# First batch's K through three places, V weights before query weights, GpSimd's mask and residuals at other places in its order

## The chip, the cores and the metric

One core of a Trainium2 chip runs the whole kernel in one launch. The metric is the device time of that launch in microseconds (us); the kernel before is shown with the median of three runs and with one profiled execution.

## The reference, cut to what matters

Eight sequences of 100 rows x 512 attend to a context of 722 rows x 512 with 16 heads of 32. Two layers follow one another, each a cross attention and a feed-forward network:

```python
q = heads(norm(x) @ Wq.T + bq); k = heads(ctx @ Wk.T + bk); v = heads(ctx @ Wv.T + bv)
p = softmax(q @ k.T / sqrt(32) + mask)      # the mask in layer 0 only
x = x + tanh(g) * (p @ v)                   # layer 1 has an output projection Wo
x = x + tanh(g) * ffn(norm(x))              # layer 0: ternary, 512-2048-2048-2048-512; layer 1: quantized gated
```

## The kernel before

Every engine has its own program, written out by hand, with semaphores between them (`w.wait_ge(sem, n)`). Every matrix product is made of three: each operand is split in a high part (rounded to the type fp32r, on ScalarE) and a low part (what is left, a subtraction on VectorE or GpSimd), and TensorE adds high x high, high x low, low x high (`PAIRS`).

The program runs `attention(0)`, the units of the first feed-forward network, `attention(1)`, and the second network. The change is in what both `attention(L)` do before their loop over 64 pairs of heads; it is called the opening below. In it TensorE computes, one after another, jobs of 12 matmuls each:

- `K00, K01, K10, K11, K20, K21, K30`: K of batch 0 for the groups of four heads g = 0 to 3, each in two halves of the 722 columns (384 and 338). `K10` is group 1, half 0. `K31` is done later, in the loop.
- `V0` to `V4`: V of batch 0, 128 context rows each, 12 matmuls of 512 columns.
- `turn_x(b)`: the normalized input rows of sequence b, turned by four transposes; `query(half)`: the query projection of four sequences, 48 matmuls of 400 columns.

A job's result goes to one of two PSUM banks in turn (5, 7), so that a job waits until the job two before it has been read out by `low_job` (semaphore `v_job`). It is read by ScalarE (`high_job`, K also gets its bias) and then by VectorE (`low_job`). High and low part of K land in the one pair of tiles `m.kst`, from which SyncE's queue stores them to DRAM (`store_k` to `kd`); `load_k` reads them back in another layout (`KS`). Since there is one `m.kst`, the next group's `high_job` for the same half waits for the store of the last (semaphore `d_kd`):

```python
i = 4 * j[1] + j[2]
if i:
    w.wait_ge(d_kd[j[3]][(i - 1) % 4], kd_done(L, i - 1))
```

All DMAs in question are issued by SyncE in a fixed order, with its waits in between. In layer 0 that order is context and K weights (0 to 3), rest of the context, x of sequences 0 to 3, weights 4 to 7 (Wq), x of 4 to 7, weights 8 and 9 (Wv), store K00, the mask's rows, store K01, weights 10 and 11, store K10, context of batch 1, store K11, and so on. `split_w(i)` is the split of weight tile i: ScalarE's high part (line 1548), VectorE's low part (line 1099), or, for the tiles in `BY_POOL`, GpSimd's (`low_wq`, line 1966). The raw tiles sit in six places, so weight i + 6 is loaded over weight i.

The norm's statistics are `stats_x` (VectorE, lines 1258 and 1260), its roots `input_roots` (GpSimd, ten small instructions for four sequences at a time, from line 1948 to 1962), and `normal_x` (VectorE, line 1264) applies them. `mask` is prepared by GpSimd for layer 0 right at the start. In layer 1, `scaled_out` (VectorE, line 1251) and `add_residual` (GpSimd, line 1974) finish the feed-forward network's last sum while the K jobs run. Behind the query, `high_q`, `low_q` (GpSimd) and `spread_q` (twelve DMAs of SyncE, line 629) bring it to the layout in which `scores` reads it.

Of the kernel before, what the change touches and what calls it, by code (L numbers as in the profile page):

```python
# [18 lines left out]
KT = 6  # L19
# [75 lines left out]
def turned_at(i):  # L95

    if i == NP - 1:
# [121 lines left out]
def flamingo_kernel(nc, t, out):  # L219
    top = ExitStack()  # L220
    with top:
# [86 lines left out]
        for L in range(2):  # L308
# [10 lines left out]
            V = [at(f"V{z}_{L}", o[f"V{z}"], [128, KT * 2 * D], F32R) for z in range(2)]  # L319
            m.QS = at(f"QS_{L}", o["QS"], [98, 2, H, S], F32R)  # L320
# [9 lines left out]
            m.wq = [V[1][:, 2048 * c:2048 * c + 2048].rearrange("p (k n) -> p k n", k=4) for c in (0, 1)]  # L330
            m.xT = [PT[:, 1600 * c:1600 * c + 1600].rearrange("p (k n) -> p k n", k=4) for c in (0, 1)]
# [3 lines left out]
            tail = at(f"xt_{L}", o["V1"] + 16384, [128, 4, D])  # L335
# [77 lines left out]
        def wait_low_w(w, L, i):  # L413

            if i in BY_POOL:
                w.wait_ge(g_wl, 2 * L + BY_POOL.index(i) + 1)
            else:
                w.wait_ge(v_wl, 10 * L + i + 1 - (2 if i > BY_POOL[-1] else 0))

# [29 lines left out]
        def _(e):  # L449
            w = Waits(e)  # L450
            def attention(L):
# [6 lines left out]
                if L == 0:  # L458
# [24 lines left out]
                    load_k(L, m, 0, 1)  # L483
                    spread_q(L, m, 0)
                else:
# [13 lines left out]
                    store_x(5)  # L499
                    store_k(L, m, *K30[1:])  # L500
                    for n in (6, 7):
                        store_x(n)
# [7 lines left out]
                    load_k(L, m, 0, 1)  # L510
                for k in range(4):
                    load_ctx(L, m, 1, 1, k)
# [61 lines left out]
            def load_w(L, m, i):  # L574
                if i >= 6:
                    wait_low_w(w, L, i - 6)
                e.dma_start(m.stage[i % 6], t[f"{('wk', 'wq', 'wv')[i // 4]}{L}"][:, i % 4, :]).then_inc(d_w[i % 6], 16)
# [15 lines left out]
            def store_k(L, m, b, g, half):  # L593
# [6 lines left out]
                for c in range(2):  # L600
                    e.dma_start(kd[n % 4, c][:, off:off + size],
                                raw32(m.kst[c][:, off:off + size])).then_inc(d_kd[half][n % 4], 16)
# [68 lines left out]
        def _(e):  # L671
# [12 lines left out]
            def attention(L):  # L684
# [3 lines left out]
                def job(j):  # L688
# [4 lines left out]
                    for k in range(4):  # L693
                        wait_ctx(w, L, j[1], half, k)
                        wait_low_w(w, L, (0 if j[0] == "k" else 8) + k)
# [116 lines left out]
                def query(half, groups=range(4)):  # L812
                    for g in groups:
                        bank = (2, 3, 4, 6)[g]
                        w.wait_ge(v_xt, 8 * L + 4 * half + 4)
                        for k in range(4, 8):
# [18 lines left out]
                for j in (K01, K10, K11, K20, K21, K30):  # L835
# [3 lines left out]
                job(V0)  # L839
                turn_x(2)  # L840
                turn_x(3)
                job(V1)
# [3 lines left out]
                job(V2)  # L846
# [234 lines left out]
        def _(e):  # L1081
# [10 lines left out]
            def attention(L):  # L1092
                m = rooms[L]
                wlow = {0: m.wk, 1: m.wq, 2: m.wv}
# [14 lines left out]
                def low_job(j):  # L1109
                    o = job_out(m, j, ring_bank(L, j))  # L1110
                    w.wait_ge(a_job, NJOB * L + JOB[j] + 1)
                    if j[0] == "k":
                        off, n = HALF[j[3]]
                        bias = bcol(f"bk{L}", j[2])
                        e.scalar_tensor_tensor(m.kst[1][:, off:off + n], o, bias, raw32(m.kst[0][:, off:off + n]),  # L1115
# [158 lines left out]
                if L == 0:  # L1274
# [4 lines left out]
                    low_job(K00)  # L1279
                    low_job(K01)  # L1280
# [5 lines left out]
                    split_w(4)  # L1286
                    split_w(5)
                    low_job(K11)
                    low_job(K20)
                    split_w(8)  # L1290
                    split_w(9)
# [3 lines left out]
                    low_job(K30)  # L1295
                    split_w(10)
# [901 lines left out]
```

## Time and profile before

| | |
|---|---|
| median of 3 runs | 1657.96 us (1657.34 to 1658.47) |
| the profiled execution's own time | 1650.54 us |
| its span, first to last instruction | 1648.7 us |
| TensorE busy (matmul) | 1587.4 us, 96% |
| VectorE, ScalarE, GpSimd busy | 1034.7, 969.6, 394.4 us |
| mean granted TensorE clock | 0.988 of full |
| chain that ended last | TensorE 88%, VectorE 4%, ScalarE 2%, DMA 2% |

Busy is the sum of an engine's instructions. The chain is followed back from the last instruction, at each step to what released it. The granted clock is 1.00 at 2.4 GHz and 0.50 at 1.2 GHz; a figure between is a mean over the stretch. The rows on which the prediction rests are in a section of their own, further on.

### The profile page before, as it was taken

Reading aid. Unit: us, or ns where it says so; the run is one execution under the profiler, and the core shown is the slowest. Engines: PE = TensorE matmul, PEld = TensorE weight load, DVE = VectorE, ACT = ScalarE, POOL = GpSimd, SP = SyncE. Lnnn points to the kernel's source line nnn. Section 1 sums busy time; section 2 is a strip of 40 time slices with the busy share of each in tenths; the row PEclk is TensorE's granted clock in tenths of the full one; section 3 lists DMA queues with packets and bytes.
Section 4 is the critical chain, followed back from the end, with each engine's and each line's share of the span. In section 5 each row is a group of like instructions: output and inputs, shape, how many; then the busy total and the mean of one; then the engine's idle time right before and its main releaser. Section 6 shows DMA issues by size and latency. Waiting matters only on the chain.

```text
span 1648.7 us, 25635 instructions
## 1 busy us (share of the span) xinstructions
PE 1587.4 (96%) x9298; PEld 1440.2 (87%) x9298; DVE 1034.7 (63%) x1833; ACT 969.6 (59%) x2007; POOL 394.4 (24%) x540
## 2 busy tenths in 40 slices
PE   4999999999997999999999999999999999999898
PEld 4888999999987999999999997789999989998654
DVE  4477777777787453223544425547777777778786
ACT  3376777677665456454544435247667767766565
POOL 3021121221224222222222222312202120213741
PEclk8899999999999999999999999999999999999999
DMA  7457766767572224555375644366676667666400
GB/s 223 104 146 192 188 172 163 195 173 185 144 207 78 96 90 164 184 179 178 99 227 199 212 147 145 111 156 175 154 191 159 180 159 190 163 152 177 155 12 29
DMA packets 146232, 257.74 MB, mean 156 GB/s; under 512 B 40916, under 2 KB 90196, under 8 KB 145968
## 3 DMA queue, kind: packets, MB, share of 16 engines
q1 hardware_dynamic: 145648, 255.79, 55.3%
q8 instruction: 85, 1.39, 0.4%
q14 instruction: 51, 0.42, 0.1%
q10 hardware_dynamic: 448, 0.14, 0.0%
HBM read 187.46 MB, written 58.57 MB: 149 GB/s over the span
## 4 chain that ended last, share of the span: by engine, by line
PE 88%; DVE 4%; ACT 2%; DMA 2%; issue 1%; POOL 1%; SPq 1%; DVEq 0%; ACTq 0%; POOLq 0%
PE ps L998 32%; PE ps L703 16%; PE ps L699 14%; PE ps L765 8%; PE ps L753 8%; PE ps L739 2%; PE ps L742 2%; PE ps L939 2%; DMA kd<-ksl 1%; PE ps L952 1%; PE ps L825 1%; PE ps L864 1%; PE ps L741 1%; PE ps L740 1%; ACT P L1593 1%
## 5 line engine op out<-in xcount | busy, mean ns | idle before, releaser
L998 PE MATMUL ps<-ah_f,wh_f 128*128 128x400 f32 (+1 forms) x1296 | 443.7, 343 | 0.9 <-issue 0.8
L998 PE MATMUL ps<-al_f,wh_f 128*128 128x400 f32 (+1 forms) x1296 | 442.2, 342 | 0.0
L1489 DVE TENSOR_TENSOR wl_f<-raw_f,wh_f 128x1024 fp32r<-128x1024 f32 x85 | 103.8, 1223 | 239.0 <-POOL wh_f L2133 239.0
L1914 POOL TENSOR_TENSOR cxl<-raw,cxh 128x384 fp32r<-128x384 f32 (+1 forms) x112 | 105.7, 965 | 619.0 <-ACT cxh L1556 619.0
L998 PEld LDWEIGHTS ps<-ah_f,wh_f 128*128 128x128 f32 x1296 | 243.5, 188 | 2.4 <-issue 1.5
L998 PEld LDWEIGHTS ps<-al_f,wh_f 128*128 128x128 f32 x1296 | 243.9, 188 | 0.0
L1127 DVE TENSOR_REDUCE nmax<-ps 100x1 f32<-100x722 f32 x256 | 220.6, 903 | 33.0 <-PE ps L741 29.4
L1593 ACT ACTIVATE P<-ps,nmax 100x722 f32<-100x722 f32 x256 | 219.9, 861 | 31.0 <-DVE nmax L1127 30.8
L1602 ACT ACTIVATE PT<-ps 128x400 fp32r<-128x400 f32 x384 | 166.5, 505 | 78.6 <-PE ps L753 77.4
L1848 ACT ACTIVATE raw_f<-wl_f 128x1024 f32<-128x1024 f32 x88 | 93.4, 1062 | 178.9 <-DVE wl_f L1489 178.9
L1133 DVE TENSOR_TENSOR PT<-ps,PT 128x400 fp32r<-128x400 f32 x384 | 196.3, 566 | 3.2
L699 PE MATMUL ps<-cxh,wkh 128*128 128x338 f32 (+1 forms) x512 | 174.9, 342 | 22.2 <-DVE ksl L1115 11.9
L2133 POOL CAST wh_f<-raw_f 128x1024 fp32r<-128x1024 f32 x85 | 92.3, 1086 | 341.8 <-PE ps L998 339.2
L699 PE MATMUL ps<-cxh,wkl 128*128 128x338 f32 (+1 forms) x512 | 170.0, 332 | 0.0
L699 PE MATMUL ps<-cxl,wkh 128*128 128x338 f32 (+1 forms) x512 | 169.1, 330 | 0.0
L703 PE MATMUL ps<-wvh,cxh 128*128 128x512 f32 (+1 forms) x384 | 160.4, 418 | 4.8 <-DVE ksl L1115 2.7
L765 PE MATMUL ps<-PT,V 128*128 128x400 f32 (+1 forms) x768 | 162.4, 347 | 2.2 <-DVE QT L1146 1.4
L753 PE MATMUL ps<-ident,P 100*128 100x100 f32 (+1 forms) x1536 | 155.8, 252 | 5.3 <-DVE PT L1133 4.1
L753 PEld LDWEIGHTS ps<-ident,P 100*128 100x128 f32 (+1 forms) x1536 | 145.7, 139 | 16.2 <-DVE PT L1133 4.5
L1115 DVE SCALAR_TENSOR_TENSOR ksl<-ps,cols,ksh 128x384 fp32r<-128x384 f32 (+1 forms) x128 | 75.6, 591 | 134.0 <-ACT ksh L1566 133.9
L703 PE MATMUL ps<-wvh,cxl 128*128 128x512 f32 (+1 forms) x384 | 151.9, 396 | 0.0
L703 PE MATMUL ps<-wvl,cxh 128*128 128x512 f32 (+1 forms) x384 | 151.5, 395 | 0.0
(188 smaller groups left out, 2596.8 us busy)
## 6 DMA issues: line engine op xcount, KB each, us to landing
KS<-kd SPq DMA_DIRECT2D x192, 361.0 KB
raw_f<-in_h SPq DMA_DIRECT2D x64, 512.0 KB, 4.1
raw_f<-in_gud SPq DMA_DIRECT2D x48, 512.0 KB, 4.5
raw<-in_ctx SPq DMA_DIRECT2D x64, 192.0 KB, 3.7
kd<-ksh SPq DMA_DIRECT2D x64, 192.0 KB, 2.2
kd<-ksl SPq DMA_DIRECT2D x64, 192.0 KB, 2.5
raw_f<-in_w SPq DMA_DIRECT2D x24, 512.0 KB, 3.7
raw<-in_ctx SPq DMA_DIRECT2D x64, 169.0 KB, 4.4
```

The lines of the kernel that those rows point to most:

```text
L699: ins = e.matmul(o, m.wk[x][:, k, 128 * j[2]:128 * j[2] + 128], m.cx[y][:, k, off:off + n], start=(k == 0 and c == 0), stop=(k == 3 and c ...
L703: ins = e.matmul(o, m.cx[y][:, k, 128 * kt:128 * kt + KM[kt]], m.wv[x][:, k, :], start=(k == 0 and c == 0), stop=(k == 3 and c == 2))
L753: ins = e.transpose(ps[0:KM[kt], bank, o:o + S], m.P[0:S, (2 * i + h) % 3, 128 * kt:128 * kt + KM[kt]], ident[0:S, 0:S])
L765: ins = e.matmul(o, m.V[b % 2][0:r, kt, g, 128 * pr:128 * pr + 128], m.PT[0:r, i % 2, :, kt, :], start=(kt == 0), stop=(kt == KT - 1))
L998: return e.matmul(o, p, q, start=start, stop=stop)
L1127: e.tensor_reduce(m.nmax[0:S, c:c + 1], scores_of(n), AX.X, ALU.max, negate=True).then_inc(v_max, 1)
L1133: e.tensor_tensor(lo, ps[:, bank, 0:400].rearrange("p (k n) -> p k n", k=2), raw32(hi), ALU.subtract).then_inc(v_t, 1)
L1489: e.tensor_tensor(wl[:, z, :], raw[:, r, :], raw32(wh[:, z, :]), ALU.subtract).then_inc(v_ul, 1)
L1593: e.activation(m.P[0:S, n % 3, :], scores_of(n), ACT.Exp, bias=m.nmax[0:S, c:c + 1], accum_out=m.rs[0:S, r:r + 1]).then_inc(a_exp, 1)
L1602: e.activation(m.PT[:, i % 2, 0, 2 * x:2 * x + 2, :], ps[:, bank, 0:400].rearrange("p (k n) -> p k n", k=2), ACT.Copy).then_inc(a_t, 1)
L1848: e.activation(raw[:, r, :], raw32(wl[:, z, :]), ACT.Abs, accum_out=low[:, z, 0:1]).then_inc(a_raw, 1)
L1914: e.tensor_tensor(m.cx[1][:, k, off:off + n], m.raw[:, k, off:off + n], raw32(m.cx[0][:, k, off:off + n]), ALU.subtract).then_inc(g_cx, 1)
```

## The change

For batch 0 of either layer, K of groups 1 and 2 gets tiles of its own (`m.kst0`, in room that V and the turned probabilities use later), so that only `K30` waits for a store (that of group 0). The weights are numbered K, V, query instead of K, query, V, so tiles 4 to 7 are Wv and 8 to 11 Wq, and GpSimd's two are 10 and 11. TensorE's order becomes K00 K01 K10 K11 K20 K21, V0, turns 0 and 1, V1, turns 2 and 3, V2, query(0), turns 4 and 5, K30, turns 6 and 7, V3, query(1). In layer 0 ScalarE and VectorE split tiles 4 to 7 straight behind K00 and tiles 8 to 11 behind turns 0 and 1; SyncE's order there follows. GpSimd makes the mask once the first context is split (`v_cx`), and in layer 1 adds six residuals instead of four ahead of the first roots.

```diff
-FIRST = ([("k", 0, g, half) for g in range(3) for half in range(2)] + [("k", 0, 3, 0)] +
-         [("v", 0, kt) for kt in range(KT - 1)])
-K00, K01, K10, K11, K20, K21, K30, V0, V1, V2, V3, V4 = FIRST
+FIRST = ([("k", 0, g, half) for g in range(3) for half in range(2)] + [("v", 0, kt) for kt in range(3)] +
+         [("k", 0, 3, 0)] + [("v", 0, kt) for kt in range(3, KT - 1)])
+K00, K01, K10, K11, K20, K21, V0, V1, V2, K30, V3, V4 = FIRST
-ADDED = (0, 1, 2, 3, 5, 7, 4, 6)
-BY_POOL = (6, 7)
+ADDED = (0, 1, 2, 3, 4, 5, 7, 6)
+BY_POOL = (10, 11)
+            m.kst0 = [[y[:, z + 722 * c:z + 722 * c + T] for c in (0, 1)] for y, z in ((PT, 3200), (V[0], 4096))]
+        def kst_of(m, b, g):
+            return m.kst if b or g in (0, 3) else m.kst0[g - 1]
...
@@ SyncE, layer 0, behind x of 0 to 3 and weights 4 to 7
-                    for b in range(4, 8):
+                    store_k(L, m, *K00[1:])
+                    store_k(L, m, *K01[1:])
+                    for b in (4, 5):
                         load_x(m, b)
-                    load_w(L, m, 8)
-                    load_w(L, m, 9)
-                    store_k(L, m, *K00[1:])
+                    store_k(L, m, *K10[1:])
+                    for b in (6, 7):
+                        load_x(m, b)
                     for c in range(2):
                         w.wait_ge(g_mask, c + 1)
                         e.dma_start(mrow[:, c, :], raw32(m.KS[0:B, 0, c, :])).then_inc(d_mrow, 16)
-                    store_k(L, m, *K01[1:])
-                    load_w(L, m, 10)
-                    load_w(L, m, 11)
-                    store_k(L, m, *K10[1:])
-                    for k in range(4):
-                        load_ctx(L, m, 1, 0, k)
                     store_k(L, m, *K11[1:])
+                    for i in range(8, 12):
+                        load_w(L, m, i)
+                    store_k(L, m, *K20[1:])
+                    store_k(L, m, *K21[1:])
                     w.wait_ge(d_mrow, 32)
                     load_k(L, m, 0, 0)
-                    store_k(L, m, *K20[1:])
-                    store_k(L, m, *K21[1:])
-                    store_k(L, m, *K30[1:])
+                    for k in range(3):
+                        load_ctx(L, m, 1, 0, k)
                     load_k(L, m, 0, 1)
                     spread_q(L, m, 0)
+                    store_k(L, m, *K30[1:])
+                    load_ctx(L, m, 1, 0, 3)
...
@@ VectorE, layer 0
                     low_job(K00)
+                    for i in range(4, 8):
+                        split_w(i)
                     low_job(K01)
...
@@ VectorE, layer 1
-                    for i in (4, 5, 8, 9, 10, 11):
+                    for i in range(4, 10):
+                        if i == 7:
+                            w.wait_ge(p_u, 87)
                         split_w(i)
...
@@ VectorE, both layers
                     for b in range(4):
                         normal_x(b)
+                low_job(V0)
                 turned_x(0)
                 turned_x(1)
-                low_job(V0)
+                if L == 0:
+                    split_w(8)
+                    split_w(9)
+                low_job(V1)
                 turned_x(2)
                 turned_x(3)
-                low_job(V1)
                 for b in range(4, 8):
                     stats_x(b)
+                low_job(V2)
                 for b in range(4, 8):
                     normal_x(b)
...
@@ ScalarE
-                        if i:
-                            w.wait_ge(d_kd[j[3]][(i - 1) % 4], kd_done(L, i - 1))
+                        if i >= 3:
+                            last = 0 if i == 3 else i - 1
+                            w.wait_ge(d_kd[j[3]][last % 4], kd_done(L, last))
...
                 if L == 0:
                     w.wait_ge(d_const, 48)
                     high_job(K00)
+                    for i in range(4, 8):
+                        split_w(i)
+                    for j in (K01, K10, K11, K20, K21):
+                        high_job(j)
...
+                high_job(V0)
+                turned_x(0)
+                turned_x(1)
+                if L == 0:
                     for i in range(8, 12):
                         split_w(i)
+                high_job(V1)
...
@@ GpSimd
                 if L == 0:
+                    w.wait_ge(v_cx, 8)
                     w.wait_ge(d_mask, 16)
...
-                    for n in range(4):
+                    for n in range(6):
                         add_residual(n)
                     input_roots(0)
-                    for n in range(4, 8):
+                    for n in range(6, 8):
                         add_residual(n)
```

## Rows read from the trace of the kernel before

**Rows 1.** Waits, first 60 us: engine, line, releaser: us in total, times, longest.
```profile
ACT ksh L1566 <- DMA kd<-ksl: 22.2, 4, 7.3
PE ps L699 <- DVE ksl L1115: 11.5, 2, 8.1
```

**Rows 2.** Timeline of TensorE, first 70 us: start, us, what, idle before.
```profile
19.09 0.31 PE L699 MATMUL ps<-cxh,wkh 128*128 128x338 f32 x1
...
29.23 0.69 PE L699 MATMUL ps<-cxh,wkh 128*128 128x384 f32 x1 [8.13 <-DVE ksl L1115]
...
33.24 0.34 PE L699 MATMUL ps<-cxh,wkh 128*128 128x338 f32 x1
...
55.53 8.90 PE L825 MATMUL ps<-PT,V 128*128 128x400 f32 x48
```

**Rows 3.** Chain that ended last, first 120 us: start, us, what.
```profile
17.32 10.55 DMA kd<-ksl
...
68.39 0.69 PE ps L681 x8
69.09 2.80 PE ps L703 x12
...
101.03 2.10 PE ps L699 x12
```

**Rows 4.** Timeline of ScalarE, first 75 us.
```profile
14.53 0.58 ACT L1566 ACTIVATE ksh<-ps,cols 128x384 fp32r<-128x384 f32 x1
...
19.25 0.63 ACT L1548 ACTIVATE V<-QT 128x512 fp32r<-128x512 f32 x1 [1.52 <-DMA QT<-in_wq]
```

**Rows 5.** Timeline of VectorE, first 75 us.
```profile
15.14 0.62 DVE L1115 SCALAR_TENSOR_TENSOR ksl<-ps,cols,ksh 128x384 fp32r<-128x384 f32 x1
...
48.22 1.28 DVE L1099 TENSOR_TENSOR wvl<-QT,wvh 128x512 fp32r<-128x512 f32 x2
```

**Rows 6.** SyncE's issue of weights 4 to 7, in its timeline.
```profile
9.40 1.78 SPq L577 DMA_DIRECT2D QT<-in_wq x4
```

**Rows 7.** DMA issues, short stretches: KB, us to landing (weight 7, weight 9, store K00).
```profile
QT<-in_wq SPq DMA_DIRECT2D x1, 256.0 KB, 11.3
...
QT<-in_wv SPq DMA_DIRECT2D x1, 256.0 KB, 12.4
...
kd<-ksh SPq DMA_DIRECT2D x1, 192.0 KB, 8.7
```

**Rows 8.** TensorE in one stretch: us, busy, matmuls, granted clock, DMA share, GB/s.
```profile
40.00:46.60 6.60, 5.57 (x20) 0.51 1.00 243
```

**Rows 9.** TensorE's waits from 1050 to 1105 us (layer 1's opening).
```profile
PE ps L703 <- DVE ksl L1115: 2.7, 1, 2.7
...
PE ps L681 <- DVE P L1264: 0.6, 1, 0.6
PE ps L699 <- DVE ksl L1115: 0.4, 1, 0.4
```

**Rows 10.** Instructions of line 1264, `normal_x`: ns min/median/max, first and last start.
```profile
L1264 DVE TENSOR_SCALAR P<-res_f,mv,rq x4: 1479/1484/1498, 1066.5 to 1070.7; 100x512 f32<-100x512 f32 x4
L1264 DVE TENSOR_SCALAR xt<-res_f,mv,rq x4: 537/538/545, 1087.5 to 1088.9; 100x512 f32<-100x512 f32 x4
```

**Rows 11.** Timeline of GpSimd, 1050 to 1075 us.
```profile
1054.20 5.05 POOL L1974 TENSOR_TENSOR res_f<-res_f,tmp 100x512 f32<-100x512 f32 x4 [12.43 <-DVE tmp L1251]
1062.82 0.26 POOL L1948 TENSOR_SCALAR rq<-mv 100x4 f32<-100x4 f32 x1 [3.56 <-DVE mv L1260]
...
1066.42 5.51 POOL L1974 TENSOR_TENSOR res_f<-res_f,tmp 100x512 f32<-100x512 f32 x4
```

**Rows 12.** SyncE's issue of the spread query, in its timeline.
```profile
66.81 5.82 SPq L629 DMA_DIRECT2D QS<-qh x8
72.67 2.54 SPq L629 DMA_DIRECT2D QS<-ql x4
```

**Rows 13.** DMA issues from 66 to 76 us: KB, us to landing.
```profile
QS<-ql SPq DMA_DIRECT2D x4, 50.0 KB, 2.0
```

More of the change, by code:

```diff
@@ L498, in attention @@
                     store_k(L, m, *K21[1:])
-                    store_x(5)
-                    store_k(L, m, *K30[1:])
-                    for n in (6, 7):
+                    for n in range(5, 8):
                         store_x(n)
@@ L510, in attention @@
                     load_k(L, m, 0, 1)
+                    store_k(L, m, *K30[1:])
                 for k in range(4):
@@ L601, in store_k @@
                     e.dma_start(kd[n % 4, c][:, off:off + size],
-                                raw32(m.kst[c][:, off:off + size])).then_inc(d_kd[half][n % 4], 16)
+                                raw32(kst_of(m, b, g)[c][:, off:off + size])).then_inc(d_kd[half][n % 4], 16)
             def load_k(L, m, b, g):
@@ L815, in query @@
                         w.wait_ge(v_xt, 8 * L + 4 * half + 4)
-                        for k in range(4, 8):
+                        for k in range(8, 12):
                             wait_low_w(w, L, k)
@@ L834, in attention @@
                     w.wait_ge(v_res, 2)
-                for j in (K01, K10, K11, K20, K21, K30):
+                for j in (K01, K10, K11, K20, K21, V0):
                     job(j)
@@ L838, in attention @@
                 turn_x(1)
-                job(V0)
+                job(V1)
                 turn_x(2)
                 turn_x(3)
-                job(V1)
+                job(V2)
                 query(0)
@@ L845, in attention @@
                 turn_x(5)
-                job(V2)
+                job(K30)
                 turn_x(6)
@@ L1335, in attention @@
                 turned_x(5)
-                low_job(V2)
+                low_job(K30)
                 turned_x(6)
@@ L1573, in high_job @@
                         if L and j[1] == 0:
-                            w.wait_ge(g_res, B)
+                            w.wait_ge(g_res, (2, 4, 7, 8)[min(j[2], 3)])
+                        if j[1] == 0 and j[2] >= 4:
+                            for h in range(2):
+                                w.wait_ge(d_kd[h][2], kd_done(L, 2))
                         e.activation(high_columns(m, j), o.rearrange("p (g r n) -> p g r n", g=4, r=2),
@@ L1601, in high_turned @@
                             w.wait_ge(p_pv, NP * L + i - 1)
+                        if i == 1:
+                            for h in range(2):
+                                w.wait_ge(d_kd[h][1], kd_done(L, 1))
                         e.activation(m.PT[:, i % 2, 0, 2 * x:2 * x + 2, :],
@@ L1660, in high_query @@
                         w.wait_ge(p_q, 8 * L + 4 * half + g + 1)
-                        for i in (7, 11):
+                        for i in (9, 11):
                             wait_low_w(w, L, i)
@@ L1677, in attention @@
                     high_job(K00)
-                    high_job(K01)
-                    split_w(4)
-                    split_w(5)
-                    high_job(K10)
-                    split_w(6)
-                    split_w(7)
-                    high_job(K11)
-                    high_job(K20)
-                    split_w(8)
-                    split_w(9)
-                    high_job(K21)
-                    high_job(K30)
-                    split_w(10)
-                    split_w(11)
-                else:
                     for i in range(4, 8):
                         split_w(i)
-                    w.wait_ge(p_u, 87)
+                    for j in (K01, K10, K11, K20, K21):
+                        high_job(j)
+                else:
+                    for i in range(4, 12):
+                        split_w(i)
+                    for j in (K00, K01, K10, K11, K20, K21):
+                        high_job(j)
+                high_job(V0)
+                turned_x(0)
+                turned_x(1)
+                if L == 0:
                     for i in range(8, 12):
                         split_w(i)
-                    for j in (K00, K01, K10, K11, K20, K21, K30):
-                        high_job(j)
-                turned_x(0)
-                turned_x(1)
-                high_job(V0)
+                high_job(V1)
                 turned_x(2)
                 turned_x(3)
-                high_job(V1)
+                high_job(V2)
                 high_query(0)
@@ L1712, in attention @@
                 turned_x(5)
-                high_job(V2)
+                high_job(K30)
                 turned_x(6)
```

35 lines of the change are left out of this document (14 added, 21 removed).

## Prediction

> **What bounds the kernel now.** I read the page first: TensorE is busy for 96% of the span and carries 88% of the chain that ended last. So the kernel is bound by TensorE, and a change to the order around it can gain only where TensorE stands still or runs at its lower clock, or lose by making more of that. Next the waits of the first 60 us. ScalarE stood 22.2 us, in four waits, for stores of K's low part, and TensorE 11.5 us for VectorE's low part of K [rows 1]. The reader is to see one chain in these two rows: the one pair of tiles for K is not free until its store to DRAM has landed, so ScalarE can't read out the next group, so VectorE can't finish it, so the PSUM bank isn't free. TensorE's timeline shows where it hurts: K11 starts at 19.09, K20 not before 29.23 after 8.13 us of nothing, and even query(0) starts only at 55.53 [rows 2]. The chain says what was late: the store of K00, issued at 17.32, took 10.55 us [rows 3], behind the loads that were issued ahead of it. The same openings, layer 0 and layer 1, are all that the edit touches; the loops behind them are TensorE's.
>
> **Layer 0, the sum.** I compare from K11's start (19.09) to the end of V3. V3 is the row that starts at 69.09 and takes 2.80, so it ends at 71.9 [rows 3]: 52.8 us. Both orders hold the same work there. At full clock it is K11, K20, K21 and K30, 2.10 for a half of 384 columns and 338/384 of it, 1.85, for the other [rows 3], 7.9 in all; four V jobs of 2.80, 11.2; four pairs of turns at 0.69, 2.8; query(0), 8.9 [rows 2]. Sum 30.8. So 22.0 us are lost today.
>
> What is lost after the change:
> - *Waits for stores: none up to K21.* Groups 0, 1 and 2 have tiles of their own. K30 waits for K00's store, which by then is 30 us old.
> - *A new wait.* ScalarE's four splits of weights 4 to 7 now stand ahead of its reading of K01. Queued behind them are K01, K10 and K11; VectorE has the same order. Today the first of the four tiles is waited for at 19.25 already [rows 4]. The four loads are issued from 9.40 on, 0.45 apart, and nothing ahead of them in SyncE's order changes [rows 6]; the last, issued at 10.8, lands 11.3 us later, at 22.1 [rows 7]. Then ScalarE splits it (0.63 [rows 4]) and reads K01 (about the same), while VectorE takes half of 1.28 for its split and then 0.62 for K01's low part [rows 5]: K01 is done at 24.0. TensorE finishes K10 at 19.1 and needs K01's bank for K11, so it stands still for 4.9 us.
> - *Lower clock.* After 8.13 us of nothing K20 took from 29.23 to 33.24, 4.0 us instead of 2.10 [rows 2, 3]: 0.48 us are lost per us at the low level. Later the clock stood at 0.51 for 6.6 us on end although TensorE worked in 5.57 of them [rows 8]. A stall of 4.9 us lies between no fall and these; bounds 0 to 7 us, so 0 to 3.4 lost. I take 5.6 us, 2.7 lost, because the stall is nearer to the one of 8.13 and a slow stretch may also outlast one job.
> - *Small gaps* between jobs: 0.5 (0 to 1).
>
> After K11 I find nothing late: K20's bank needs K10, read right behind K01; stats and roots end before VectorE comes to the first normalized row behind K21; weights 4 to 7 are long split when V0 starts. Lost: 4.9 + 2.7 + 0.5 = 8.1, against 22.0. **Layer 0 gains 13.9 us**, and V3 ends at about 58.
>
> *Weights 8 to 11* move behind the store of K11, which waits for VectorE (28.8 by the same walk), and behind four x tiles and six K stores. Issued from 29.8 to 31.7, they must be split by ScalarE (four times 0.57) ahead of V1's reading at 39.0, and by GpSimd (1.3 each) before query(0) at 42.7. With a landing after 5 us there is a margin of 1 to 2 us, so they cost nothing; with the 11.3 of [rows 7] they would cost (rival C). x of 4 to 7 is needed at about 41 only; *the mask* is then made at 15 to 20 us, where VectorE has a hole, and its two small DMAs gate nothing before the first scores; its old place held up one low part of the context at 6.8 us, but the next K weight hadn't landed yet, so nothing is gained there. The store of K30, now behind the twelve query DMAs, serves a load two pairs later.
>
> One rule speaks on the new wait. Today four x loads and two weight loads are issued behind weights 4 to 7 and share the engines with them; after the change they come later. The store of K00 landed after 8.7 us at 25.2, ahead of weight 9, issued before it and landed after 12.4 us at about 27.4 [rows 7], so order of issue is not order of landing. The Trainium skill (DMA: Bandwidth & Descriptors, section on queues, rings and completion order) says that on each DMA engine descriptors are consumed in ring order. By that rule later loads don't hold back weight 7, and the sum stands; by the other reading weight 7 lands up to 3 us earlier (rival B).
>
> **Layer 1, the sum.** TensorE's waits are 2.7 for V0's bank, 0.6 for the second turn and 0.4 for a K bank [rows 9], 3.7 together. The first two come from `normal_x`: four of them took 1484 ns each, against 538 for the other four [rows 10], while GpSimd added residuals at 1066.42 to 1071.9 [rows 11], and V0's bank waited behind them on VectorE. After the change GpSimd adds six before the roots: 6 x 1.26 from 1054.20 is 1061.8, still ahead of the roots' start at 1062.82, which wait for VectorE [rows 11], so the two moved ones are free; two remain beside `normal_x`, and two of its four stay slow. V0 no longer stands behind them, since K21's low part comes first; the second turn waits until 1069.6 where V0 ends at 1068.1, less one turn: 0.8. **Gain 3.7 - 0.8 = 2.9** (bounds 1.0, if all four stay slow, and 3.7). VectorE's split of weight 7 now waits for unit 86 of the network before, while units 86 and 87 still keep TensorE busy: nothing.
>
> **First scores.** They need the spread query: 2.4 us from query(0)'s end (55.53 + 8.90 = 64.4) to the first issue at 66.81, 8.4 of issuing [rows 12], 2.0 to land [rows 13], 12.8 together. TensorE's cover is now two pairs of turns, K30 instead of V2, V3 and three quarters of a query: 1.4 + 2.1 + 2.8 + 6.7 = 13.0, 0.7 less than before. That is barely enough; I take 0.2 lost over both layers (0 to 2).
>
> **Total.** 13.9 + 2.9 - 0.2 = 16.6. The profiled execution's own 1650.54 becomes 1633.9; it ran 7.4 us under the median shown, so for the median 1657.96 - 16.6 = **1641.4 us**, 1.0% less. Moved work that stands in the openings is passed on in full, because from the first scores on TensorE has hardly a gap.
>
> **Rivals.**
> - **A, as worked out** (0.60): 1641.4. Its own range, from the clock (0 to 3.4), layer 1 and the first scores: 1638 to 1645.
> - **B, weights 4 to 7 land earlier** (0.14), since less is queued with them: weight 7 at about 19.5, a stall of 2.3 instead of 4.9 and a shorter slow stretch, 3.3 gained on top: 1638. For it: the landing order in [rows 7]; against it the even steps in which the four land.
> - **C, a new wait at the query weights** (0.17). They take 11.3 us like their forerunners and land at 43.0. ScalarE's splits stand ahead of V1's reading and of turns 2 and 3, so query(0) starts at 45.7 instead of 42.7, 3.0 lost, and 1.8 more if that brings a slow stretch of 3.7 us: 1646.2. For it: their issue now follows stores and x tiles that drain at the same time. Against it: by 30 us the first rush of loads is over.
> - **D, no change** (0.04): the opening gets shorter, but the first scores then wait for K or the query, or the loop's context loads come late, and the time is given back: 1658.
> - **E, slower** (0.03). Place: ScalarE's queue at weight 7, with all of K behind it. Each us that it lands later is a us lost. Weight 7 would have to land after 22.1 + 16.6 = 38.7; at 42 the time is 1661. Nothing queued ahead of it has grown, which is why I give it so little.
> - Mixtures of A and C with smaller losses hold the rest (0.02).
>
> **Range.** B's lower end and A without any slow stretch go to 1636; C with some more of D's losses to 1650. Outside lie most of D, E and a little more: two in ten at most. A measurement here tells about 0.2% (3.3 us) from nothing: faster 0.94, within it 0.03, slower 0.03.
>
> **What would show it.** Right: no wait of ScalarE for stores in the first 60 us; TensorE's only large gap from 19 to 24, ended by K01's low part; query(0) at about 43; V3's end at 58; in layer 1 `normal_x` with two slow and two fast, and three TensorE waits less. Wrong: a wait of ScalarE for the query weights near 37 to 43, a gap ahead of the first scores, or a gap at 19 that ends well before or after 24.

## The result, and the profile after

The changed kernel takes 1635.99 us (median of 4 runs: 1630.64, 1631.64, 1640.34, 1640.59) against 1657.65 us for the kernel before beside it. The ratio is 0.9868, 95% interval 0.9828 to 0.9908. Forecast was 1641.4 with a range from 1636 to 1650: the direction came out, and so did the place of the gain, but the gain is larger than forecast, and the median lies 0.01 us under the range's lower end.

The profiled execution's own time is 1640.59 us, its span 1638.8, its mean granted clock 0.986; before it was 1650.54, 1648.7 and 0.988. From its page, the busy time of each engine:

```profile
PE 1592.8 (97%) x9298; PEld 1446.9 (88%) x9298; DVE 1031.3 (63%) x1833; ACT 970.8 (59%) x2007; POOL 393.7 (24%) x540
```

The same 9298 matmuls are busy 5.4 us longer than before. That is the first sign that some of the gain of the opening was paid back at the lower clock. Waits of TensorE in the first 60 us, answering to [rows 1] (us in total, times, longest):

```profile
PE ps L704 <- DVE cxl L1111: 9.3, 2, 7.1
PE ps L704 <- DVE ksl L1121: 3.6, 1, 3.6
```

ScalarE has no wait for a store left; its waits for DMAs are now these:

```profile
ACT wvh L1554 <- DMA QT<-in_wv: 3.8, 1, 3.8
ACT cxh L1562 <- DMA raw<-in_ctx: 3.1, 4, 2.1
ACT wkh L1554 <- DMA QT<-in_wk: 1.1, 2, 0.7
ACT V L1554 <- DMA QT<-in_wq: 0.4, 1, 0.4
```

The wait of 11.5 us for K's low part [rows 1] has become one of 3.6, and what stands behind it is ScalarE's wait for weight 4. TensorE's timeline, answering to [rows 2], with the first scores (L744) as its last row:

```profile
22.68 0.65 PE L704 MATMUL ps<-cxh,wkh 128*128 128x338 f32 x1 [3.64 <-DVE ksl L1121]
...
39.86 8.90 PE L830 MATMUL ps<-PT,V 128*128 128x400 f32 x48
...
61.75 0.39 PE L744 MATMUL ps<-KS,QS 98*100 98x512 f32 x1
```

ScalarE's timeline, answering to [rows 4], shows the four splits without a pause and K01 behind them:

```profile
18.89 2.51 ACT L1554 ACTIVATE wvh<-QT 128x512 fp32r<-128x512 f32 x4 [3.82 <-DMA QT<-in_wv]
21.31 0.53 ACT L1573 ACTIVATE ksh<-ps,cols 128x338 fp32r<-128x338 f32 x1
```

query(0) starts 15.7 us earlier than in [rows 2]. Layer 0's first scores start at 61.75 instead of 78.28: **16.5 us gained**. Their position was read in both timelines; the stretches below divide the openings (columns as in [rows 8]). First the kernel before, from K11 to V3's end, and layer 1 from its first K matmul to its first scores:

```profile
19.09:71.90 52.81, 37.98 (x178) 0.81 0.53 146
1052.98:1102.11 49.13, 45.11 (x248) 1.00 0.54 144
```

Then the changed kernel, the same work:

```profile
19.04:55.36 36.32, 32.62 (x177) 0.95 0.80 198
1042.32:1088.49 46.17, 44.49 (x248) 1.00 0.54 148
```

In layer 0 TensorE stands still for 3.7 us instead of 14.8, and it is busy 5.4 us less with the same jobs, because less of them runs at the lower clock. Layer 1's opening is 3.0 us shorter. Together the openings gain 19.5 us.

But the two profiled spans differ by 9.9 us only. From layer 0's first scores to layer 1's first K matmul the changed kernel took 980.6 us (61.75 to 1042.32), the one before 974.7. The loss of 5.9 us lies where the attention loop hands over to the network. (Another 3.7 us were lost from layer 1's first scores to the end, 550.3 us against 546.6. There too it is the clock: in the four stretches of 20 us that begin 400 us behind those scores it was 0.83, 0.90, 0.93 and 0.92, before 0.91, 0.83, 1.00 and 1.00.) TensorE in the changed kernel:

```profile
480.00:500.00 20.00, 14.44 (x92) 0.84 0.07 20
500.00:520.00 20.00, 17.89 (x100) 0.76 0.34 104
520.00:540.00 20.00, 20.00 (x103) 0.89 0.29 102
```

and before, where these stages come some 15 us later:

```profile
500.00:520.00 20.00, 14.80 (x87) 0.83 0.07 21
520.00:540.00 20.00, 17.91 (x124) 1.00 0.39 130
```

Both have a pause of 2.1 us there, for the same releaser. After it the changed kernel's matmuls of 200 columns took 0.41 us each:

```profile
514.15 0.93 PE L808 MATMUL ps<-ident,x 100*128 100x100 f32 x4 [2.11 <-DVE x L1242]
...
515.10 0.41 PE L1003 MATMUL ps<-al_f,wh_f 128*128 128x200 f32 x1
```

and those of the kernel before 0.27:

```profile
529.61 0.56 PE L803 MATMUL ps<-ident,x 100*128 100x100 f32 x4 [2.10 <-DVE x L1236]
...
530.24 0.28 PE L998 MATMUL ps<-ah_f,wh_f 128*128 128x200 f32 x1
530.35 0.27 PE L998 MATMUL ps<-al_f,wh_f 128*128 128x200 f32 x1
```

It is the same pause, one time with the clock at its lower level (1.2 GHz) behind it and one time without. Nothing in the diff touches this place, so the question for the experiments is twofold: which part gives the 19.5 us, and does the clock at the hand-over belong to the change or differ from run to run.

### The profile page after: what moved, and what is told of

It is laid out like the page before. It is cut to its first block, busy times and chain, and to the rows that moved or that the text cites. A ratio compares the mean times of both kernels' runs of the same rounds, so it can differ in the third digit from the quotient of the medians.

```text
span 1638.8 us, 25637 instructions
## 1 busy us (share of the span) xinstructions
PE 1592.8 (97%) x9298; PEld 1446.9 (88%) x9298; DVE 1031.3 (63%) x1833; ACT 970.8 (59%) x2007; POOL 393.7 (24%) x540
## 4 chain that ended last, share of the span: by engine, by line
PE 92%; DVE 3%; ACT 2%; issue 1%; POOL 1%; DMA 1%; SPq 1%; DVEq 0%; ACTq 0%; POOLq 0%
PE ps L1003 32%; PE ps L708 16%; PE ps L704 15%; PE ps L758 8%; PE ps L770 8%; PE ps L830 2%; PE ps L944 2%; PE ps L744 2%; PE ps L747 2%; PE ps L957 1%; PE ps L869 1%; PE ps L746 1%; PE ps L745 1%; DMA QT<-in_wv 1%; ACT P L1603 1%
## 5 line engine op out<-in xcount | busy, mean ns | idle before, releaser
L770 PEld LDWEIGHTS ps<-PT,V 128*128 128x128 f32 (+1 forms) x768 | 141.2, 191 | 3.3 <-DVE QT L1152 0.2
```

Source lines behind the costliest of these rows:

```text
L770: ins = e.matmul(o, m.V[b % 2][0:r, kt, g, 128 * pr:128 * pr + 128], m.PT[0:r, i % 2, :, kt, :], start=(kt == 0), stop=(kt == KT - 1))
```

## Experiments

The ratio is always to the kernel before, run beside it. "First scores" is the start of layer 0's first scores in the profile (78.28 before, 61.75 changed), "opening 1" the stretch from layer 1's first K matmul to its first scores (49.13 before, 46.17 changed).

**1. The old queue behind weights 4 to 7.** The prediction let weights 4 to 7 land as late as before, because later loads were not to hold them back; rival B let them land earlier, because less is queued with them. Here the x tiles 4 to 7 and two more weights (1.3 MB) go right behind them again, as before the change:

```diff
                     for i in range(4, 8):
                         load_w(L, m, i)
+                    for b in range(4, 8):
+                        load_x(m, b)
+                    load_w(L, m, 8)
+                    load_w(L, m, 9)
                     store_k(L, m, *K00[1:])
                     store_k(L, m, *K01[1:])
-                    for b in (4, 5):
-                        load_x(m, b)
                     store_k(L, m, *K10[1:])
-                    for b in (6, 7):
-                        load_x(m, b)
...
-                    for i in range(8, 12):
+                    for i in range(10, 12):
                         load_w(L, m, i)
```

> The changed kernel, with SyncE's loads of x 4 to 7 and of weights 8 and 9 put back right behind weights 4 to 7, as in the kernel before. In the changed kernel ScalarE ran its four splits of weights 4 to 7 from 18.89 to 21.4 us without a pause, and K11 started at 22.68. Theory B (later loads hold the earlier ones back): the four splits have pauses again, the last weight lands near 22.1, K11 starts near 24.0, and the first scores come 1.3 to 3 us later than the changed kernel's 61.9. Theory A (order in the rings, later loads don't matter): splits and K11 as in the changed kernel within 0.3 us, and the earlier landing has another cause.

Measured: 1642.11 us in one run (clock 0.986); first scores at 63.34, 1.6 later. Weight 7's landing (DMA issues, KB, us to landing), first with the old queue:

```profile
QT<-in_wv SPq DMA_DIRECT2D x1, 256.0 KB, 11.3
```

and in the changed kernel:

```profile
QT<-in_wv SPq DMA_DIRECT2D x1, 256.0 KB, 9.6
```

The first of the four took 10.0 against 9.1. ScalarE's splits with the old queue:

```profile
19.76 1.26 ACT L1554 ACTIVATE wvh<-QT 128x512 fp32r<-128x512 f32 x2 [4.55 <-DMA QT<-in_wv]
21.27 0.63 ACT L1554 ACTIVATE wvh<-QT 128x512 fp32r<-128x512 f32 x1 [0.25 <-DMA QT<-in_wv]
22.42 0.63 ACT L1554 ACTIVATE wvh<-QT 128x512 fp32r<-128x512 f32 x1 [0.52 <-DMA QT<-in_wv]
```

The last split starts at 22.42, which is the sum's 22.1 plus a little, and K11 at 24.31 after 4.5 us: this is nearly the stall that the prediction worked out (24.0, 4.9). Two single traces can't size this, since landings vary from run to run. Over all 13 traces of this case, weight 7 landed after 9.5 to 10.8 us with the new order behind it (nine traces, mean 10.1) and after 10.7 to 11.3 with the old one (four traces, mean 11.1); the first of the four tiles landed after 9.1 to 10.2 and after 9.5 to 10.0, which is no clear difference. In the seven traces with the changed kernel's loads and splits K11 started at 22.50 to 23.59, here at 24.31. So loads issued *later* on the same queue spread the four landings and hold back the last by about 1 us. The Trainium skill (DMA: Bandwidth & Descriptors, section on queues, rings and completion order) has descriptors consumed in ring order on each engine, but adds that a later one may finish its write before an earlier one. The prediction took the first half for a statement on landing times, and in these rows the landing of weight 7 did depend on what was issued behind it.

**2. The places alone.** The kernel before with groups 1 and 2 of K in tiles of their own; all orders as before.

```diff
+            m.kst0 = [[y[:, z + 722 * c:z + 722 * c + T] for c in (0, 1)] for y, z in ((PT, 3200), (V[0], 4096))]
...
-                        if i:
-                            w.wait_ge(d_kd[j[3]][(i - 1) % 4], kd_done(L, i - 1))
+                        if i >= 3:
+                            last = 0 if i == 3 else i - 1
+                            w.wait_ge(d_kd[j[3]][last % 4], kd_done(L, last))
```

> The kernel before, with only the three places for K of batch 0 (the waits for stores of K10 to K21 gone), every order as before. Theory P (the stores' waits were nearly all of the loss): first scores in layer 0 near 62 to 66 us instead of 78.4, so 12 to 16 us of the 16.5 gained. Rival O (the order of the weights is needed too): ScalarE then waits for weights 8 and 9, which land at 26 to 27 us, ahead of K21, and SyncE's loads of 10 and 11 wait behind VectorE; V0 waits for them, and the first scores come at 68 us or later, a gain under 10 us. Layer 1: at most 1 us of gain, since VectorE's slow normalized rows still stand ahead of V0's bank.

Measured: 1640.28 us, ratio 0.9904 (0.9884 to 0.9924). First scores at 62.66: 15.6 of the 16.5 us. TensorE's waits in the first 60 us, behind its first K matmul:

```profile
PE ps L704 <- DVE PT L1121: 2.4, 2, 1.5
PE ps L686 <- DVE P L1270: 2.0, 1, 2.0
PE ps L686 <- DVE xt L1270: 0.2, 1, 0.2
```

In layer 1 the wait of 2.7 us for V0's bank is still there, as in [rows 9], so the places give nothing. Opening 1 came out at 51.8 us, even 2.7 longer than before, and that is mostly the clock:

```profile
1063.42 0.79 PE L708 MATMUL ps<-wvh,cxh 128*128 128x512 f32 x1 [2.72 <-DVE V L1121]
1064.01 0.63 PE L708 MATMUL ps<-wvh,cxl 128*128 128x512 f32 x1
```

A V matmul takes 0.39 to 0.40 at full clock, here 0.63; the clock fell behind this pause of 2.72 us and did not behind the pause of 2.7 in [rows 9].

**3. The order alone.** The changed kernel with the one old pair of tiles.

```diff
         def kst_of(m, b, g):
-            return m.kst if b or g in (0, 3) else m.kst0[g - 1]
+            return m.kst
...
-                        if i >= 3:
-                            last = 0 if i == 3 else i - 1
-                            w.wait_ge(d_kd[j[3]][last % 4], kd_done(L, last))
+                        if i:
+                            w.wait_ge(d_kd[j[3]][(i - 1) % 4], kd_done(L, i - 1))
```

> The changed kernel with one pair of tiles for K again (and its waits for stores), every order as changed. Theory P: K11 to K21 wait 3 to 5 us each for a store, the first scores in layer 0 come at 70 us or later, so most of the gain is gone. Rival O (the stores were late only because of the loads ahead of them, which the new order moves): each store lands in 2 to 3 us, the first scores come at 64 to 67 us, and the places are worth 2 to 5 us only.

Measured: 1636.16 us, ratio 0.9869 (0.9853 to 0.9886), which can't be told from the changed kernel's. First scores at 64.36, 2.6 later; opening 1 46.4. The stores of K01, issued behind the weights' rush instead of inside it (KB, us to landing):

```profile
kd<-ksh SPq DMA_DIRECT2D x1, 169.0 KB, 1.8
kd<-ksl SPq DMA_DIRECT2D x1, 169.0 KB, 2.1
```

Before they took 7.0 and 9.5. The stores of K10 took 2.9 and 3.5 us here, those of K11 3.5 and 5.6. ScalarE waits for a store once in the first 62 us, ahead of its reading of K21:

```profile
ACT ksh L1572 <- DMA kd<-ksl: 3.8, 1, 3.8
```

K11 starts at 22.58, as early as in the changed kernel. What that wait costs TensorE is one of 1.5 us ahead of the first turn; most of the rest of the 2.6 is the clock, which here stayed at its lower level into K20 (to 28.0, against 26.1). So one pair of tiles is nearly enough when its stores are this quick, and the two parts of the change are almost each sufficient in layer 0 (15.6 and 13.9 of 16.5 us), and they don't add up. In layer 1 the order (with the residuals) gives 2.7 of the 3.0 us without the places.

**4. Residuals four and four.** GpSimd in layer 1 adds four ahead of the roots, as before.

```diff
-                    for n in range(6):
+                    for n in range(4):
                         add_residual(n)
                     input_roots(0)
-                    for n in range(6, 8):
+                    for n in range(4, 8):
```

> The changed kernel with four residuals ahead of layer 1's first roots and four behind, as before. My prediction's view: all four of the first normalized rows run beside GpSimd (near 1480 ns each), and layer 1's opening (first K matmul to first scores, 46.3 us in the changed kernel) gets 1 to 2 us longer. Rival (the order alone took the waits away, since V0's bank no longer stands behind those rows): the rows are slow, but TensorE does not wait more, and the opening stays within 0.3 us of 46.3.

Measured: 1636.43 us in one run; opening 1 47.15, 1.0 us longer, at the low end of what was expected. Instructions of `normal_x` (as in [rows 10]), first of this kernel:

```profile
L1270 DVE TENSOR_SCALAR P<-res_f,mv,rq x4: 1485/1499/1512, 1056.1 to 1060.4; 100x512 f32<-100x512 f32 x4
```

then of the changed one, where two are slow and two are not:

```profile
L1270 DVE TENSOR_SCALAR P<-res_f,mv,rq x4: 535/1012/1495, 1055.9 to 1059.1; 100x512 f32<-100x512 f32 x4
```

**5. The changed kernel again.** No edit; it shows what differs between executions.

> The changed kernel once more, unchanged, in more rounds, beside the two others of this call. Theory G (the spread of its times comes from falls of TensorE's clock at the hand-over from one stage to the next, and is not in the openings): times again from about 1630 to 1641 us, the longer ones with the lower mean clock (0.986 against 0.994), while the first scores of layer 0 stay at 61.8 +- 0.5. Rival: the spread comes from the openings (loads that land differently), and the first scores move by several us from run to run.

Measured: 1636.44 us (1635.19 to 1640.67), ratio 0.9883 (0.9865 to 0.99). First scores 61.83, opening 1 46.18: the openings repeat within 0.1 us. The stretch between them was 979.2 us. The fall behind the pause is there again, though it begins only 1 us behind it, with the first matmuls still at 0.28. TensorE in the 40 us around it (columns as in [rows 8]):

```profile
500.00:540.00 40.00, 37.12 (x206) 0.87 0.31 103
```

Over all eight timed runs the time goes with the mean granted clock: 1631 at 0.993 and 0.994, 1635 to 1637 at 0.991, 1640 to 1641 at 0.986. Their mean is 1636.5, that of the 13 runs of the kernel before beside them 1657.0: 20.5 us, against 19.5 of the openings.

**6. The splits behind K10.** The one new wait, taken away: ScalarE and VectorE read K01 and K10 before the splits of weights 4 and 5, K11 before those of 6 and 7.

```diff
                     high_job(K00)
-                    for i in range(4, 8):
-                        split_w(i)
-                    for j in (K01, K10, K11, K20, K21):
-                        high_job(j)
+                    high_job(K01)
+                    high_job(K10)
+                    split_w(4)
+                    split_w(5)
+                    high_job(K11)
+                    split_w(6)
+                    split_w(7)
+                    high_job(K20)
+                    high_job(K21)
```

(and VectorE nearly likewise: splits of weights 4 and 5 behind K10, of 6 and 7 behind K20, its statistics of sequences 2 and 3 behind K11)

> The changed kernel with the four splits of the V weights spread behind K10 and K11 (ScalarE: K00 K01 K10, splits 4 5, K11, splits 6 7, K20 K21; VectorE: K00 K01, stats 0 1, K10, splits 4 5, K11, stats 2 3, K20, splits 6 7, K21). My theory: the new wait of 3.64 us for K01 and the slow stretch behind it are a price of the order of the splits. Without it K11 starts at 18.9, the clock stays up, a wait of about 1 us appears ahead of the first turn (roots are ready at 28 us), and the first scores come 4 to 5 us earlier than 61.75, at about 57. Rival: V's weights land at 18.9 to 21 us and hold K11's reading, so that K20 or K21 waits instead, and 1 us or less is gained.

Measured: 1634.39 us, ratio 0.9851 (0.9833 to 0.9869), mean 1633.0; first scores at 57.99, 3.8 us earlier. The means alone (5 and 8 runs that spread over 7 and 10 us) would not show a gain of 3.5 clearly; the trace does. No K job waits; TensorE's only wait after the context is this one:

```profile
PE ps L686 <- DVE P L1270: 0.6, 1, 0.6
```

**7. The pause at the hand-over, filled.** 11 matmuls of 400 columns, whose results nothing reads, in the pause of 2.1 us ahead of the last sequence's turn, at the hand-over from layer 0's attention to the network. Nothing is left out of the computation.

```diff
+                    ring_free(("xn", B - 1))
+                    for _ in range(11):
+                        e.matmul(ps[:, ring_bank(L, ("xn", B - 1)), 0:HN], wh[:, 0, 0:128], act[0][:, 0, 0:HN], start=True,
+                                 stop=True)
                     turn_normal(B - 1)
```

> The changed kernel with 11 extra matmuls of 400 columns (results unused) in the gap of 2.1 us ahead of the last sequence's turn at the hand-over from layer 0's attention to the network (514 us in the changed kernel's profile, where the clock then stood at 0.50 for 10 us). They do no needed work and take 1.9 us that TensorE would wait anyway. Theory G: no fall of the clock behind that gap, so the stretch from the first scores of layer 0 to the first K matmul of layer 1 (980.4 us in the changed kernel, 974.7 in the kernel before) comes out at 974 to 977, and the longest times shrink to about 1636. Rival (the falls belong to other waits, or the extra power makes one): no difference, 1630 to 1641 as before.

Measured: 1632.57 us (1630.81 to 1635.35), ratio 0.9849 (0.9835 to 0.9862), mean 1632.6 against 1636.5; the clock was 0.991 to 0.995 in the five runs. The stretch between the openings took 974.6 us. TensorE at the hand-over, from its timeline and, below, by stretches:

```profile
511.66 2.17 PE L899 MATMUL ps<-ah_f,wh_f 128*128 128x400 f32 x11
513.94 0.56 PE L808 MATMUL ps<-ident,x 100*128 100x100 f32 x4
...
500.00:520.00 20.00, 18.74 (x129) 1.00 0.32 112
520.00:540.00 20.00, 20.00 (x112) 1.00 0.36 121
```

The stretch behind layer 1's first scores, which this edit doesn't touch, took 550.1 us here, as long as in the changed kernel's profile (550.3).

**8. GpSimd's mask at the start again.**

```diff
                 if L == 0:
-                    w.wait_ge(v_cx, 8)
                     w.wait_ge(d_mask, 16)
```

> The changed kernel with the mask made at the start again, as before. My prediction: VectorE's first low part of the context takes 2.05 us again instead of 0.55 and TensorE's first matmul starts at 8.9 instead of 7.1, but the second K weight lands later anyway, so that K00 ends at the same time and the first scores stay within 0.5 us of 61.75. Rival: the later start costs its 1.8 us in full, first scores at 63.5.

Measured: 1632.19 us in one run; the first K matmul starts at 9.10 instead of 7.08, the second group of them at 10.73 like before (10.68), and the first scores at 62.90, 1.15 later. That is between the two expectations. In the runs without this edit the first scores moved by up to 1.0 us too (61.75, 61.83, 62.71 in experiment 7), so how much of the 1.15 is the mask's stays open; the time, lower than the changed kernel's, doesn't speak against it, since its clock was 0.993. This trace shows something else: the pause at the hand-over isn't filled (2.10 us), and the clock behind it stayed up.

```profile
500.00:540.00 40.00, 36.67 (x229) 1.00 0.36 116
```

The stretch between the openings took 974.6 us and that behind the second one 546.7, against 974.7 and 546.6 in the kernel before. So the change lengthens neither; what the changed kernel's two own profiles lose there, they lose by the clock.

**9. Splits behind K10 and the filled pause together.**

> Both edits in one kernel: the splits of the V weights spread behind K10 and K11, and the 11 extra matmuls in the gap at the hand-over. If they add up: the opening as in e5 (first scores at 58.0), the stretch to layer 1's first K matmul 974 to 977, times from 1627 to 1632, some 7 us under the changed kernel's mean of 1636.5. Rival (the extra matmuls only had luck in five runs): times from 1629 to 1636, as with the splits alone.

Both edits are as above. Measured: **1627.11 us** (1626.59 to 1629.56), ratio 0.9822 (0.9806 to 0.9839), clock 0.994 to 0.996. First scores 58.59, stretch between the openings 976.3. The means fall by 3.5 for the splits alone, 3.9 for the pause alone and 8.9 for both, so they add up; the 1.5 us beyond the sum are no more than these means vary. This kernel beats both.

**10. The filled pause in the kernel before.**

> The kernel before, with only the 11 extra matmuls in the gap at the hand-over. Theory G (the fall of the clock there is independent of the change, and costs the kernel before as much): 1650 to 1653 us, 3 to 5 us under the kernel before. Rival (the gap only matters after the change, by its moment): no difference, 1654 to 1659.

Measured: 1651.7 us in 12 runs, 1655.55 in 17 of the kernel before; ratio 0.998 (0.9967 to 0.9992). The pause costs the kernel before about as much (3.9 between the medians, 3.5 between the means) as the changed one; the interval only just leaves out no change. Its opening 1 took 50.75 us, 1.6 more than in the kernel before, though nothing was edited there: behind the pause of 2.73 us ahead of V0 the clock fell, as in experiment 2.

**11. The same 11 matmuls where TensorE is busy.** A control: 11 matmuls of 384 columns ahead of a K job of batch 3, in the loop of layer 0.

```diff
                         wait_low_w(w, L, (0 if j[0] == "k" else 4) + k)
+                        if L == 0 and k == 0 and j == ("k", 3, 0, 0):
+                            for _ in range(11):
+                                e.matmul(o, m.wk[0][:, 0, 0:128], m.cx[0][:, 0, 0:384], start=True, stop=True)
```

> A control: the changed kernel with 11 extra matmuls of 384 columns in a stretch where TensorE is busy and never waits (ahead of batch 3's first K job in layer 0). Theory G (it is the gap's filling that helps): 1.9 us of work more and the same spread, 1632 to 1643 us, mean 1638.4. Rival (any added work or a shift of the later stages by 2 us changes the clock's luck): times as low as with the matmuls in the gap, 1631 to 1635.

Measured: 1643.14 us (1642.3 to 1643.44), ratio 0.9926 (0.9911 to 0.994), clock 0.987 to 0.989. Put elsewhere, the same work brings nothing, and the clock falls behind the pause again (1.7 us behind its end, for some 7 us):

```profile
500.00:520.00 20.00, 15.09 (x107) 1.00 0.28 100
520.00:540.00 20.00, 20.00 (x102) 0.83 0.26 80
```

Its median is 6.6 us above the changed kernel's mean, and the 11 matmuls account for about 2 of them. The rest goes with the clock, in all four runs; whether by chance or because the loop behind them is shifted isn't settled, so this control doesn't show what a shift alone does.

All traces together say most on the pause. In the ten in which it isn't filled, the clock fell at its end or within 2 us behind it in eight, to its lower level for 7 to 14 us; the stretch between the openings took 979.2 to 982.1 us in them (the longest with the 2 us of extra matmuls in it). In the other two (the kernel before and experiment 8) it didn't fall, and the stretch took 974.7 and 974.6. In the three with the pause filled (experiments 7, 9 and 10) it never fell, and the stretch took 974.5 to 976.3. What decides between a fall and none behind the unfilled pause stays open.

## Why the prediction was right on the mechanism, and which step was off

- **What bounds the kernel, and where the loss sits: right.** ScalarE's wait for stores is gone, query(0) moved from 55.53 to 39.86 (forecast "about 43"), and outside the openings only the clock differs (experiment 8).
- **No wait for stores up to K21: right** (no such wait in the first 60 us). What the prediction missed is that the order alone would nearly do it as well, since K's stores land in 1.8 to 5.6 us once the loads are out of their way (experiment 3).
- **The new wait: right in place and releaser, too large.** The term "TensorE needs K01's bank for K11, so it stands still for 4.9 us" measured 3.64. The step that failed is the landing of weights 4 to 7, taken over from the trace of before as 11.3 us although the queue behind them had changed. They landed after 9.1 to 9.6. That is rival B's mechanism, at half of its size, and experiment 1 brought nearly the forecast stall back (4.5 us, K11 at 24.31). Once weight 7 no longer decides, ScalarE's four splits do: they run without a pause for 2.5 us from the landing of weight 4 (18.89). B overlooked this. By its own rows, four splits of 0.63 from 19.25 [rows 4] end at 21.8 and K01 at 23.0, so its stall of 2.3 us was not to be had without an earlier weight 4.
- **Lower clock: the second term too large.** 5.6 us at the lower level were taken, 2.7 lost. K11 ran at the low level for its 3.45 us (clock 0.52) and K20 at the full one: 1.6 lost. With 0.3 for small gaps the opening loses 5.5 us where 8.1 were forecast, and layer 0 gains 16.5 where 13.9 were. In the other traces with this order of loads and splits the stall was 3.6 to 4.8 us, so part of this difference is what single executions vary by.
- **Weights 8 to 11 and rival C: right, and refuted.** The query weights landed after 5.9 us, and ScalarE waited 0.4 for them.
- **Layer 1: right in size, 2.96 against 2.9, though one of its terms is another.** The residuals are worth 1.0 (experiment 4), about half of what they were taken for (2.9, or 1.0 if all four rows stay slow: 1.9). The wait for V0's bank is gone, and the turn waits 0.9. In return there is a wait that the prediction doesn't have, ahead of the last pair of turns:

```profile
1075.63 1.28 ACT L1714 ACT_TABLE_LOAD   x1
1076.93 0.20 ACT L1714 ACTIVATE warm<-ident 128x1 f32<-128x1 f32 x1
1077.04 0.88 ACT L1546 ACTIVATE PT<-ps 128x400 fp32r<-128x400 f32 x2
```

  ScalarE loads its table for the exponential there, and TensorE's cover for it is now K30 (2.1 us) and no longer V2 (2.8), so TensorE waits 0.77 for the tile behind it at 1078.28. That it comes out even is in part luck: TensorE is also 0.6 us less busy in the same work behind fewer pauses. And with the old order this opening took 49.13, 50.75 and 51.82 us in three traces (the kernel before, experiments 10 and 2), by whether the clock fell behind the pause at V0, so its gain can be larger than 2.96.
- **First scores: right.** 6.4 us from V3's end to the scores, before and after; the cover of 13.0 us held, 0.2 was charged.
- **The sum.** 16.6 forecast, 19.5 measured in the openings. Of the 2.9 between them 1.3 are the stall, 1.1 the slow stretch behind it, and the rest small gaps and the first scores. So 1638.5 was to be expected from 1657.96. The other 2.5 us of the median are the four runs' clock (1631 twice, 1640 twice; the mean over eight runs is 1636.5). The range made no room for that: it held the bounds of the costs, but not the 10 us by which single executions of the same kernel differ, and its lower end stood on B's landing times as if they were the furthest thing. The sum took the clock outside the openings as the same before and after, "because from the first scores on TensorE has hardly a gap"; the pause of 2.1 us at the hand-over is such a gap, and it was not looked at.
- **E** (slower) never came near: weight 7's split ended at 21.4, not after 38.7.

## What to carry to other kernels

A landing time in the trace belongs to the queue it was read in: when the change takes loads away from behind a transfer, bound its landing from below as well; here later loads cost the last of the earlier ones about 1 us. Where two edits attack one chain (more places for a store, quicker stores), each may do nearly all of it; try them alone before keeping both. Where a kernel's time goes with the clock from run to run, as here, look in a slower profile for a pause with a fall of the clock behind it, and try to fill it, with other work or even with matmuls that nothing reads.

## What the runs showed of the hardware

- The same pause of TensorE was followed by full clock in one execution and by 1.2 GHz in another: 2.10 us without a fall before, 2.11 us with 10 us at a clock of 0.52 after (a fall in eight of ten traces), 2.7 us both ways in layer 1. With the first pause filled with 2.2 us of matmuls no fall followed in three traces, and the mean time was 3.9 us lower (8 and 5 runs; 3.5 in the kernel before, 17 and 12 runs).
- The changed kernel's stretch behind that pause, whose length and clock are read in this row:

```profile
514.00:524.60 10.60, 10.45 (x46) 0.52 0.30 97
```

- A stall of 3.64 us was followed by 3.45 us at the low level and then by the full clock, less than the 4.0 us of one job that [rows 2, 3] show behind 8.13 us:

```profile
22.68:26.13 3.45, 3.45 (x12) 0.52 0.63 207
26.13:29.00 2.87, 2.87 (x19) 1.00 0.78 264
```

- A load of ScalarE's function table took 1.28 us and the next activation started 0.02 us behind it. The Trainium skill (ScalarE: Activation LUTs, What ACT_TABLE_LOAD costs) adds a drain of 1.38 us to such a load; no gap of that size stands on either side of it in this trace.
